# Scan stage: the group's normalisation at step 3 of a slot, the input turnings and squares at other steps

## What is computed

```python
x = x + _L0_conv_ref(_ln_c(x), ...)      # window attention
t = _to_tokens(x)                        # 64 samples x 3136 tokens x 128 channels
t = t + _L0_ffn_ref(_ln_t(t), ...)       # a recurrence over the 3136 tokens
x = _from_tokens(t, x)
x = x + _L1_conv_ref(_ln_c(x), ...)      # gated complex filter, 16 repeats of one step
t = _to_tokens(x)
t = t + _L1_ffn_ref(_ln_t(t), ...)       # experts: softmax over tokens, top 8, two matmuls, scatter
```

## Time and profile before

| | us |
|---|---|
| median of 3 runs (13164.88 to 13181.59) | 13171.84 |
| the profiled execution | 13158.25 |
| its span, from first to last instruction | 13156.4 |
| scan stage, first to last tanh of the recurrence | 5291.7 to 11205.4 |
| DVE busy over the span | 10185.1 (77%) |
| ScalarE busy | 9159.4 (70%) |
| PE busy | 9385.1 (71%) |

### The profile page before, as it was taken

How to read it: one execution, slowest core, us unless ns; L and a number is a source line. 1 busy time by engine, 2 the same in 40 slices (tenths; PEclk the granted TensorE clock), 3 DMA queues, 4 the chain that set the end, 5 groups by cost and what they waited for, 6 DMA issues and landing times. The chain is left out here.

```text
span 13156.4 us, 223254 instructions
## 1 busy us (share of the span) xinstructions
PE 9385.1 (71%) x77110; PEld 6941.7 (53%) x77110; DVE 10185.1 (77%) x22621; ACT 9159.4 (70%) x21851; POOL 5332.7 (41%) x4855
## 2 busy tenths in 40 slices
PE   7888888888888887766666666666666665255544
PEld 5666666666766665544444444444444443133343
DVE  6777777777777775388888888888888889899910
ACT  6888888888888886466667666666666666477711
POOL 4444444454444444122222322222222223188866
PEclk9999999999999998676766666666767666677755
DMA  3333333333333332244444444444444444476544
GB/s 72 80 80 80 85 86 85 84 80 80 80 80 80 85 85 67 59 105 106 103 109 103 109 100 107 105 100 109 102 108 104 109 97 95 63 141 125 98 80 70
DMA packets 1451133, 1215.62 MB, mean 92 GB/s; under 512 B 65493, under 2 KB 1337368, under 8 KB 1399844
## 3 DMA queue, kind: packets, MB, share of 16 engines
q1 hardware_dynamic: 1290212, 653.81, 21.5%
q0 software_dynamic: 103232, 444.75, 18.7%
q10 hardware_dynamic: 56576, 102.79, 2.3%
HBM read 567.56 MB, written 325.32 MB: 68 GB/s over the span
## 5 line engine op out<-in xcount | busy, mean ns | idle before, releaser
L1282 PEld LDWEIGHTS s_pW<-s_XU,s_vh 128*128 128x128 f32 x6272 | 1451.6, 263 | 2039.1 <-ACT s_XU L1156 1758.7
L1282 PE MATMUL s_pW<-s_XU,s_vh 128*128 128x64 f32 x6272 | 1523.5, 336 | 1132.1 <-ACT s_XU L1156 1117.2
L1156 ACT ACTIVATE s_XU<-s_pW 128x64 f32<-128x64 f32 x3136 | 715.0, 228 | 1179.0 <-PE s_pW L1282 1146.8
L1311 PE MATMUL s_pG<-s_wg,s_XNT 128*128 128x384 f32 (+1 forms) x3200 | 1491.0, 554 | 8.2 <-ACT s_Z L1128 8.2
L414 ACT ACTIVATE KB<-pV,qkb 32x392 f32<-32x392 f32 x2048 | 1188.1, 580 | 25.0 <-PE pV L504 1.1
L254 POOL TENSOR_TENSOR SS<-SS,mx 128x784 f32<-128x784 f32 x512 | 768.8, 1502 | 800.2 <-DVE mx L347 800.1
L1172 ACT ACTIVATE s_f<-s_X,s_nmr,s_rst 128x128 f32<-128x128 f32 (+1 forms) x1600 | 654.1, 485 | 559.8 <-POOL s_nmr L862 559.8
L262 POOL TENSOR_TENSOR XR<-XR,pbias 112x512 f32<-112x512 f32 x448 | 570.5, 1274 | 665.3 <-DMA XR<-in_x_dram 665.3
L466 ACT ACTIVATE XH<-XR,nm,rs 112x128 f32<-112x128 f32 x1792 | 731.2, 482 | 104.3 <-POOL nm L273 96.0
L1269 PE MATMUL s_pN<-s_ident,s_f 128*128 128x128 f32 (+1 forms) x800 | 211.0, 418 | 826.1 <-issue 437.9
L512 PE MATMUL pS<-KB,QT 128*64 128x196 f32 x8192 | 793.7, 336 | 0.0
(11 more groups left out here) (261 smaller groups left out, 28894.7 us busy)
## 6 DMA issues: line engine op xcount, KB each, us to landing
XL<-in_x_dram SPq DMA_DIRECT2D x64, 1568.0 KB, 12.5
XR<-in_x_dram SPq DMA_DIRECT2D x64, 1568.0 KB, 18.3
x_dram<-XR SPq DMA_DIRECT2D x64, 1568.0 KB, 8.1
xh_dram<-XH SPq DMA_DIRECT2D x64, 1568.0 KB, 8.2
e_X<-out_dram SPq DMA_DIRECT2D x64, 1568.0 KB, 16.0
s_XQ<-xh_dram ACTq DMA_DIRECT2D x384, 256.0 KB, 4.5
s_X<-x_dram POOLq DMA_DIRECT2D x96, 1024.0 KB, 8.1
s_BX<-s_Dl POOLq DMA_DIRECT2D x96, 1024.0 KB, 7.0
```

The source lines that it names most:

```text
L1156: act.activation(XU[j % 2][:, t, :], pW[t // R % 2][:, B * (t % R):B * (t % R) + B], ACT.Tanh, scale=0.5).then_inc(u_sb, 1)
L1282: pe.matmul(pW[t // R % 2][:, B * (t % R):B * (t % R) + B], vh[:], before, start=False, stop=True, skip_group_check=True).then_inc(z_ps, 1)
L1311: pe.matmul(pG[i % 3][0:tc, 0:3 * C], XNT[:, i, 0:tc], wg[:], start=True, stop=True).then_inc(g_ps, 1)
```

## The change

In slots 1 to 3 of a chunk the normalisation moves from step 10 to step 3 (`first_normal`), with the turning of XN (step 4) and the copies to XNT (step 5) behind it. The turnings of the next chunk's inputs move behind them, from steps 0, 3, 6, 9 to steps 9, 11, 13, 15 (`turning`), with their evictions one step later. In slot 0 these stay where they were. In all slots the squares move: L1177 and L1178 from step 6 to 8, L1180 from 8 to 10, L1183 from 14 to 12, L1198 from 16 to 14, L1203 from 20 to 19, L1207 from 22 to 21. DVE's L1044 waits for the first square of the group instead of the first three. PE's waits for the bank pX follow the new order. In slot 0 GpSimd issues `add_x1` ahead of `add_input`. Nothing is added or removed. Since lines are added, all lines behind L764 have a number 10 higher in the changed kernel.

```diff
+        def first_normal(s):
+
+            return 10 if s == 0 else 3
+
+        def turning(s, k, after):
+
+            first, step = (0, 3) if s == 0 else (9, 2)
+            q, r = divmod(k - after - first, step)
+            return q if r == 0 and 0 <= q < NQ else None
...
             for j, s, oc, o, scan, prep in slots():
+                if oc is not None and s == 0:
+                    add_x1(oc)
                 if o is not None and o >= 1:
                     add_input(o - 1)
-                if oc is not None and s == 0:
-                    add_x1(oc)
...
-                    dve.wait_ge(am, o * NA + 3)
+                    dve.wait_ge(am, o * NA + 1)
                     did(dve.scalar_tensor_tensor(t1, d0, -2.0, t1, ALU.mult, ALU.subtract))
...
-                    if prep and k in (1, 4, 7, 10):
-                        keep_turned(j, s, k // 3)
-                    if conv and 10 <= k < 10 + NQ:
-                        q = k - 10
+                    if prep and turning(s, k, 1) is not None:
+                        keep_turned(j, s, turning(s, k, 1))
+                    if conv and 0 <= k - first_normal(s) < NQ:
+                        q = k - first_normal(s)
...
-                    if o is not None and k == 6:
+                    if o is not None and k == 8:
...
-                    if o is not None and k == 8:
+                    if o is not None and k == 10:
                         act.activation(d1, d0, ACT.Square).then_inc(am, 1)
-                    if o is not None and k == 14:
+                    if o is not None and k == 12:
...
-                    if conv and 12 <= k < 12 + NQ:
-                        q = k - 12
+                    if conv and 0 <= k - first_normal(s) - 2 < NQ:
+                        q = k - first_normal(s) - 2
...
-                    if o is not None and k == 16:
+                    if o is not None and k == 14:
...
-                    if o is not None and k == 20:
+                    if o is not None and k == 19:
...
-                    if o is not None and k == 22:
+                    if o is not None and k == 21:
...
                 if oc is not None:
-                    wait(pe, n_sb, oc * NQ)
+                    wait(pe, n_sb, (oc + (s > 0)) * NQ)
...
-                    if prep and k in (0, 3, 6, 9):
-                        turn_inputs(j, s, k // 3, oc)
-                    if conv and 11 <= k < 11 + NQ:
-                        if k == 11:
+                    if prep and turning(s, k, 0) is not None:
+                        turn_inputs(j, s, turning(s, k, 0), oc)
+                    if conv and 0 <= k - first_normal(s) - 1 < NQ:
+                        q = k - first_normal(s) - 1
+                        if q == 0:
                             if scan and s == NO - 2:
                                 pe.wait_ge(raw_d, j + 1)
-                            if prep:
-                                pe.wait_ge(xt_sb, ((j + 1) * NO + s) * NQ + NQ)
-                        turn_normal(oc, tc, k - 11)
+                            pe.wait_ge(xt_sb, min((j + 1) * NO + s + (s == 0), NCH * NO) * NQ)
+                        turn_normal(oc, tc, q)
```

## The result

The changed kernel takes 13,571.31 us (median of 4 runs, 13,554.98 to 13,580.46) against 13,168.36 for the kernel before on the same chip: a ratio of 1.0303, interval 1.0285 to 1.0321. It is 3.0% slower, 403 us. Its profiled execution took 13,554.98 us (span 13,553.1), 396.7 more than the profiled one before. The forecast was 13,690 with a range of 13,400 to 13,880: the direction is right, and the size is 119 us too much.

The account below looks back on a forecast made before the run. The scan stage was held bound by DVE and the loop through GpSimd's product and ScalarE at once. Slots 0 to 3 at -2.7, +8.8, +10.5, +5.7 gave +22.3 us a chunk, 23 chunks 513: 13,690 us, range 13,400 to 13,880.

Parts of the forecast that it names:

- The loop: Scan stage: a slot's length is R + H + W + 16.36 us, the last being DVE's remaining work after the last square.
- R: From DVE's list end (second pair of L1082) to GpSimd's last product; unchanged near 13.3 and 21.2 us in slots 1 to 3.
- H: Delay from GpSimd's last product to ScalarE's normalisations; the most they can gain: 1.70, 0.04, 4.07 us in slots 1 to 3.
- x: Growth of W in slots 1 to 3 from work now behind the normalisations; taken as 10.5 us.
- W: From the begin of the normalisations to the end of the last square; forecast 33, 34 and 30 us in slots 1 to 3.
- moved stretch: Slot 1's work from step 3 to the normalisations, plus first eviction, less 1.45 us after the last square: 9.5 us.
- upper end: Slots 1 to 3: x is 11.6 us with two of the four sets of transposes unhidden, 1.06 us each.
- the hidden work: Rival: moved work fits into idle time after the normalisations and the kernel gets faster, 13,070 us; chance 0.05.
- the ScalarE that never idles: Rival: ScalarE never idles after the normalisations, x near 2, about 13,170 us, no difference; chance 0.03.
- the early rival: Rival: denser turnings after the normalisations raise PE's clock early, x = 7.6, 13,420 us; chance 0.13.
- The first slot's term: Slot 0: x1 load 5.5 us earlier, 3.2 lost on ScalarE's lead, W -0.4: net -2.7 us.
- ScalarE's lead: ScalarE's first tanh of slot 0, 2.51 us ahead of the list end, would start 0.7 behind: 3.2 us lost.

Follow-up runs that it names:

- e7_stat_first: The changed kernel with GpSimd's three products (and slot 2's four before them) ahead of the input add in slots 1 to 3: 13,277.93 us, 1.0077 of the kernel before.
- e8_step6: The changed kernel with normalisations at step 6 instead of 3 and turnings at steps 12, 14, 16, 18 in slots 1 to 3: 13,375.75 us, 1.0155 of before.
- e5_pause: The kernel before with one more DVE wait, in slot 0 behind the statistics, until GpSimd's three products are done: 13,061.65 us, ratio 0.9919.
- e2_pool: The kernel before with only GpSimd's order in slot 0 changed, the x1 load ahead of the input add: 12,950.89 us, ratio 0.984.
- e1_move: The kernel before with only the normalisations and turnings moved in slots 1 to 3; squares, their wait and GpSimd's order as before: 13,904.85 us, ratio 1.0561.

## Why the prediction was right, and where its size was off

**The loop held.** R stayed at 13.25, 21.35 and 13.38 us in slots 1 to 3, as forecast, and H went to 0.03. So the earlier place gained 1.68, 0.01 and 4.04 us, the prediction's H. e7_stat_first confirms from the other side that R is what the loop hangs on.

**x was right, in part because its misses cancel.** W grew by 9.45, 9.81 and 11.50 us; the forecast was 10.5 in all three, from a moved stretch of 9.5 and an upper end of 11.6. The slots grew by 7.77, 9.86 and 6.73, in place of 8.8, 10.5 and 5.7: 24.36 together, forecast 25.0; the misses of the three, -1.03, -0.64 and +1.03, nearly cancel. The recurrence did not fill its idle time with the moved work, so the rivals of the hidden work and of the ScalarE that never idles fall: 25.24 us of work in 32.58.

**The clock rose later, not earlier.** PE is at 0.50 for 11.88 us after the normalisations begin and at 0.64 in the 12 us behind [the windows above], where in the earlier trace rows it was at 0.94 after 14.5. Worked out from these means, with 0.50 and 1.00 as the two levels, PE spent 23.5 of the 32.58 us of W at 1.2 GHz, and 15.5 of 23.02 before. So the early rival falls. Its premise, a denser run of PE, did not come: PE was busy for 6.35 of the 11.88 us, in the earlier trace rows for 11.62 of 14.5. The later rise was no term of the sum, and it is part of x. A rough estimate of its size comes from e8_step6: in slots 1 to 3 PE spends 3.8, 1.6 and 8.8 us less of W at 1.2 GHz there than in the change (medians), and W is 2.5, 2.3 and 3.8 us shorter; from slot 2 to slot 3 that is 1.5 us of W for 7.2 us at the lower clock, 0.2 for each. The change has 7.9 to 9.3 us more at the lower clock in each of these slots than the kernel before, so some 1.7 us of x could be the clock's. No run changes the clock alone. The prediction also read too much from the trace of before: PE is at 0.50 at the first normalisation of all 92 groups of chunks 1 to 23, but not after every wait of ScalarE (of its 436 idle times over 1 us between 5700 and 11,000 us, 180 end with PE at 2.4 GHz).

**The first slot's term failed.** It was -2.7 us and measured -7.32. By its own parts: the load of x1 landed in 8 us, and DVE had its data 8.19 us after the issue (8820.36 - 8812.17) in place of 13.6, a gain of 5.4 as forecast. ScalarE's lead before the list end shrank by 1.61 us (2.42 to 0.81), not by 3.2. The prediction held that this lead is there only because slot 3 is bound by DVE; in the changed kernel slot 3 is not, and ScalarE still starts slot 0 0.81 us ahead of the list end, where it starts slots 1 to 3 1.07 behind. Slot 3 has no copies to X2 at steps 22 and 24 behind its last square; that this is the reason was not tested. W changed by +0.11, not -0.4. And the part that was missing: the three products take 3.93 us in place of 7.88, because DVE pauses there. The prediction said that the input add would take none of the gain, since DVE needs it only after the statistics; DVE does wait 1.64 us for it, and that wait is what let GpSimd go ahead. -5.4 + 1.6 - 4.0 + 0.1 = -7.7, near the -7.32. Read as 4.6 us a chunk, 23 x 4.6 = 106 of the 119 us by which the forecast was too long. e5_pause shows the cause by itself, and e2_pool the term: -9.5 without the loss of ScalarE's lead.

**The squares** cost nothing by themselves, as forecast; they give nothing in the old order. In the new one they give 6.4 us a chunk (e1_move against the change), of which the forecast had 1.45 us a slot in x, 4.4 us.

**The waits** came as said: 7.85 us in slot 1 and 16.1 at most in slot 2, forecast 9 and 17; the one ahead of L1187 is gone, L1054 has a new one in 38 slots of 76, and DVE's last wait, at L1076 for the square of step 21, came in all 76.

## What to carry to other kernels

An instruction on an in-order engine should stand where its input is ready: put earlier than that it gains no more than the time it stood ready, and everything behind it pays the wait; here each of the two edits that put it three steps later took 2.3 to 3.8 us from W in each slot it touched. Look first for what makes the input late: this kernel held 6 us of slot 2 in four products whose result nothing needs before the next chunk, and 9.5 us of slot 0 in the order of two transfers. An engine that is off the path may still be slowed by the one on it, so the duration of a short instruction on the path should be read at two places of the trace before it is put into a sum.

## What the runs showed of the hardware

GpSimd's instructions on SBUF were held by DVE's. The product L858 of 128 x 16 took 0.21 us where DVE stood still and 2.19 where DVE worked on L939, a tensor_tensor of 128 x 2048, and it ended 0.08 us after that one; the three together took 3.5 and 7.9 us. This is not slot 0 alone. In the kernel before, L862 ends 0.08 us after the DVE instruction beside it in 98 of 100 groups (in the other two DVE stood still, and it took 0.22), and the power L860 ends 2.8 us after it in 99. So each of the three can pay for one DVE instruction; in slot 1 of the changed kernel they still take 7.30 us of R.

Short DVE instructions cost little: in e7_stat_first the four products of slot 2 came beside instructions of 0.34 us at most and the start of the statistics, and took 1.47 us in all, where in the changed kernel, beside the filter's instructions of 1.2 to 2.3 us, they take 1.19, 1.25, 1.10 and 2.18. A long DVE instruction that reads one tensor did not hold GpSimd, as the expert stage of the kernel before shows; there GpSimd also held DVE:

```profile
11608.36 3.42 DVE L1537 MAX8 e_m<-e_Lg 128x8 f32<-128x3136 f32 x1
...
11610.36 0.19 POOL L1478 TENSOR_TENSOR e_grs<-e_gvar,e_epst 128x8 f32<-128x8 f32 x1
...
11645.81 6.18 POOL L1485 TENSOR_TENSOR e_X<-e_X,e_rst 112x3584 f32<-112x3584 f32 x1
...
11645.99 6.02 DVE L1544 TENSOR_SCALAR e_ids<-e_ix,e_base 128x8 uint32<-128x8 uint32 x1
```

L1478 took 0.19 us in the middle of MAX8. L1544, which takes 0.23 us at its shortest, took 6.02 and ended 0.02 us after L1485. In the scan stage DVE was hardly held: L949 took 2.29 us though GpSimd's power L870 had begun 1.26 us before it.

The Trainium skill, "SBUF — State Buffer", section "SBUF: two separate sides", says that DVE and GpSimd share one pair of ports as an exclusive lock, and that whichever of the two begins first, a DVE instruction with two SBUF inputs against a GpSimd instruction that reads SBUF among them, holds it for its whole length. The rows of the first slot agree where DVE began first: GpSimd's product ends just after DVE's instruction does. They differ for the power, which began first and did not hold L949; why, no run here shows. Spans on GpSimd are rough in the profile, but the slot's length moved by the same 4.4 us.
